# State-space layers: decay ring 8 to 16, state ring 16 to 8, sum lag 9 to 6

## The reference, cut to what matters

```
dA = exp(dt[:, :, None] * A)
h  = h * dA + (dt * u)[:, :, None] * B[:, None, :]     # over 512 time steps
y  = sum over states of h * C  +  u * D
out = x + gate * ((y * silu(z)) @ W_out)
```

## Time and profile before

| | |
|---|---|
| median of 3 runs | 2964.96 us (2961.61 to 2968.52) |
| profiled execution | 2969.68 us, span on the core 2968.0 us |
| busy share of the span | PE 82%, DVE 73%, ACT 73%, POOL 57% |
| L1038 scan | 1024 x 1209 ns, 205.5 us idle before them |
| L1121 product h * C | 1024 x 1370 ns |
| L909 decay tile, L891 scaled row | 1024 x 715 ns, 1024 x 714 ns |
| L1300, L1285 transposes and sums | 4096 each, 628.1 and 623.3 us busy |

### The profile page before, as it was taken

One profiled execution on the slowest core, in us unless ns is written; L12 is line 12 of the kernel. 1 busy time (PEld: TensorE's weight loads), 2 busy tenths in 40 slices (PEclk: granted clock), 3 DMA queues, 4 the chain that ended last, 5 costly groups with the idle time before them and its releaser, 6 DMA issues. The chain is left out here.

```text
span 2968.0 us, 44243 instructions
## 1 busy us (share of the span) xinstructions
PE 2442.6 (82%) x14532; PEld 1664.9 (56%) x14532; DVE 2178.1 (73%) x2878; ACT 2159.3 (73%) x3593; POOL 1689.8 (57%) x1365
## 2 busy tenths in 40 slices
PE   7778578898898898637888999857888888889885
PEld 4555257777677777512333333224576666677784
DVE  4443378888888898556777776615899988998983
ACT  3333389999999999513666656547989989999993
POOL 0000078888988989650111111004989889899895
PEclk9999799999999999867999999878999999999997
DMA  3100211112112111145555544111111112112121
GB/s 106 39 28 22 73 40 45 51 60 65 39 60 67 37 53 60 38 93 81 80 87 87 82 82 76 22 55 43 44 67 60 58 53 78 61 53 74 58 68 43
DMA packets 106124, 177.01 MB, mean 60 GB/s; under 512 B 10709, under 2 KB 91405, under 8 KB 97199
## 3 DMA queue, kind: packets, MB, share of 16 engines
q1 hardware_dynamic: 101679, 161.69, 21.3%
q0 software_dynamic: 4224, 12.59, 1.3%
HBM read 139.70 MB, written 34.14 MB: 59 GB/s over the span
## 5 line engine op out<-in xcount | busy, mean ns | idle before, releaser
L1121 POOL TENSOR_TENSOR l_h<-l_h,l_c_all 128x512 f32<-128x512 f32 x1024 | 1380.7, 1370 | 184.8 <-DVE l_h L1038 168.9
L1038 DVE TENSOR_TENSOR_SCAN l_h<-l_dA,l_ps_dbu 128x512 f32<-128x512 f32 x1024 | 1218.8, 1209 | 205.5 <-PE l_ps_dbu L1300 102.1
L1300 PE MATMUL l_ps_dbu<-ident,l_dub 128*128 128x128 f32 x4096 | 628.1, 276 | 151.0 <-DVE l_h L1038 79.7
L909 ACT ACTIVATE l_dA<-l_dt,l_a_neg 128x512 f32<-128x512 f32 x1024 | 731.1, 715 | 7.0 <-issue 5.2
L891 ACT ACTIVATE l_dub<-l_duT,l_b_tok 128x512 f32<-128x512 f32 x1024 | 730.4, 714 | 2.4 <-PE l_ps_dbu L1300 2.0
L1285 PE MATMUL l_ps_y<-ident,l_h 128*128 128x128 f32 x4096 | 623.3, 275 | 11.8 <-POOL l_h L1121 8.8
L1300 PEld LDWEIGHTS l_ps_dbu<-ident,l_dub 128*128 128x128 f32 x4096 | 471.0, 141 | 205.0 <-DVE l_h L1038 112.0
L1285 PEld LDWEIGHTS l_ps_y<-ident,l_h 128*128 128x128 f32 x4096 | 485.5, 142 | 130.8 <-issue 92.4
L1795 ACT ACTIVATE l_probs<-l_ring 128x512 f32<-128x512 f32 x512 | 292.8, 598 | 261.9 <-PE l_ring L1933 260.7
L1614 DVE TENSOR_REDUCE l_q_max<-l_ring 128x1 f32<-128x512 f32 x512 | 338.4, 683 | 175.6 <-PE l_ring L1926 171.8
L1933 PE MATMUL l_ring<-l_qs,l_ks 102*128 102x512 bf16 x512 | 201.5, 398 | 59.5 <-DMA l_qs<-l_m_parts 51.4
(11 more groups left out here) (248 smaller groups left out, 2949.7 us busy)
## 6 DMA issues: line engine op xcount, KB each, us to landing
l_c_all<-c_rows_dram SPq DMA_DIRECT2D x64, 1024.0 KB, 4.8
l_res<-x_dram SPq DMA_DIRECT2D x24, 512.0 KB, 6.0
parts_dram<-l_parts SPq DMA_DIRECT2D x48, 256.0 KB, 2.9
l_qs<-parts_dram SPq DMA_DIRECT2D x48, 256.0 KB
l_ks<-parts_dram SPq DMA_DIRECT2D x48, 256.0 KB
l_x_in<-x_dram SPq DMA_DIRECT2D x16, 512.0 KB, 7.3
x_dram<-l_res SPq DMA_DIRECT2D x16, 512.0 KB, 3.1
l_x_in<-in_x SPq DMA_DIRECT2D x8, 512.0 KB, 4.3
```

What stands on the lines that cost most here:

```text
L909: act.activation(dA[:, s % DA_RING, :], dt[:, p, j, :], ACT.Exp, scale=a_neg[:, j * N + n:j * N + n + 1]).then_inc(da_ok, 1)
L1038: dve.tensor_tensor_scan(h[:, h_slot(s), :], dA[:, s % DA_RING, :], ps_dbu[:, dbu_slot(s), :], 0.0, ALU.mult, ALU.add).then_inc(scan_ok, 1)
L1121: pool.tensor_tensor(h[:, h_slot(s), :], h[:, h_slot(s), :], c_all[:, (n // C_GROUP) % 2, n % C_GROUP, :], ALU.mult).then_inc(hc_ok, 1)
L1300: last = pe.transpose(ps_dbu[:, dbu_slot(s), t * P:(t + 1) * P], dub[:, DUB_SLOTS[n], t, j * P:(j + 1) * P], ident[:])
```

## The change

The decay ring gets 16 tiles in place of 8, the state ring 8 in place of 16, so the tiles' memory stays the same in sum. The sums on PE follow six units behind in place of nine, so the skip terms of a batch are at steps 6 to 9 of PE. Since 1 - DA_RING would make the first wait on scan_ok zero or negative, that semaphore gets a start of its own, SCAN_CREDIT = 16, and the waits on it by ACT, POOL and PE are raised alike.

```
 UNITS = N * JB
-DA_RING, DBU_RING, H_RING = 8, 3, 16
-SUM_LAG = 9
+DA_RING, DBU_RING, H_RING = 16, 3, 8
+SUM_LAG = 6
 CREDIT = 8
+SCAN_CREDIT = 16
...
-                        act.wait_ge(scan_ok, b * UNITS + s + 1 - DA_RING + CREDIT)
+                        act.wait_ge(scan_ok, b * UNITS + s + 1 - DA_RING + SCAN_CREDIT)
...
-                dve.sem_inc(scan_ok, CREDIT)
+                dve.sem_inc(scan_ok, SCAN_CREDIT)
...
-                        pool.wait_ge(scan_ok, b * UNITS + s + 1 + CREDIT)
+                        pool.wait_ge(scan_ok, b * UNITS + s + 1 + SCAN_CREDIT)
...
-                        pe.wait_ge(scan_ok, b * UNITS + s + 1 - dbu_back(s) + CREDIT)
+                        pe.wait_ge(scan_ok, b * UNITS + s + 1 - dbu_back(s) + SCAN_CREDIT)
```

## The result

The changed kernel takes **3105.82 us** (median of 4 runs, 3101.01 to 3112.68); the kernel before took 2966.74 beside it (4 runs). The ratio is 1.0473, with a 95% interval of 1.0447 to 1.0498: 139 us slower. The forecast was 3068, in a range from 3035 to 3105; the result lies 0.8 us above the top of the range. The profiled execution has a span of 3102.9 us, 134.9 longer than before. In the engines' programs lines stand one further on than before: the scan is L1039, the skip term L1276, the sum L1286, the transposes L1301, y_gate L1008.

A forecast was written before the change was run, and what follows sets the result against it. DVE and PE set the pace from unit 5 to 28, ACT from there to unit 4. 12 x 7.4 + 2 x 7.1 = 103 us on the median 2964.96 gave 3068 us, range 3035 to 3105 (0.80).

The forecast's parts named there:

- the stall: Units 6 to 9: PE and DVE take turns four times per batch, so scan 9 comes 8.4 us later.
- the give-back: Before unit 11: DVE's 1.09 us idle goes, no skip term being left there, so scan 11 is only 7.4 us late.
- ACT's slack absorbs it: Rival: ACT's 5.70 us of waits per batch are slack, leaving 1.7 a batch; 2985 to 3035 us; chance 0.08.
- PE is relieved: Rival: skip terms cost nothing at step 6 and the 1.09 us stall before unit 11 goes; 2950 us; chance 0.03.
- no effect: Rival: the lag and the rings are all loose; 2965 us; chance 0.02.
- The clock: I take none.: PE's new 1.9 us idle gaps in the turns: no clock loss in the centre, 27 us for the range's top.
- the top of the range: 3105 us: 10 us a batch, with one slow turn and POOL's wait.
- clock falls at every turn: Rival: half clock in all four turns of each batch, 108 us more, 3176 us; anything over 3105 has chance 0.07.
- The turn: Units 6 to 9, scan to scan through y_gate, skip term, sum and transposes: 3.82 us, where it was 1.72.
- ACT's wait at the projection: Unit 12 (L823): projection 8.3 us later; ACT's waits at L823, L844 and L836 longer by 5 to 8 us per batch.
- Layer 3: Tap relief, at most 18 us, a third (6) taken, against POOL's wait (4.5): about cancel, taken as 0.
- The wait for POOL: Layer 3, units 53 to 63: earlier sums may wait for POOL's products, 0 to 9 us in seven batches, middle 4.5.

## Why the prediction was right, and where its size was off

**Right, with numbers.** The mechanism, its place and its sign. The lag of 6 puts skip term j ahead of transposes 6 + j, PE and DVE take turns four times in each of 14 batches, and the run with the lag alone shows it to be the whole loss. The gap of PE came at 1.90 us as forecast. The decay tiles and the states came at nothing, as forecast. The batch is longer by what the stall adds, less the give-back: ACT's waits at L824 end on projections that lie behind the stall, so the rival "ACT's slack absorbs it" (2985 to 3035) is out. "PE is relieved" and "no effect" are out by the scans that wait at L1301.

**The step that failed** is "The clock: I take none." I held one row against it: the fall at 641 followed 2.30 us of waiting, and the new gaps are 1.9. They are shorter, but the clock fell all the same, in every one of the 14 windows; I had noted "four in a row" and given it no price. The changed kernel and the same with idle transposes measure it: 3105.82 and 3075.21 us, 31 apart on two chips, ratios 1.0473 and 1.0371; on the chip of the second, the lag alone took 3105.22, 30 us more. The profiles place it: 246.3 - 222.4 = 23.9 in the turns, and 51.9 - 46.1 = 5.8 from scan 9 to 11. The 27 us that I kept for the top of the range, one slow turn a batch, was about the right size; it belonged in the centre, at 3095. By the sign that I had named for it, a granted clock of 0.5 in units 6 to 9, the rival "clock falls at every turn" came true in part; its price (3176) did not: 29 of the 56 turns took 3.93 to 3.98 us, the third of the batch above among them, and the window at 619 has 1.6 us at half clock in all (twice 0.05 x 16.45).

The Trainium skill, TensorE: Matmul & The Clock Gate, section "A second HAM failure mode: psum-queue depth-cycling", says that short idle spells between groups of matmuls make the clock swing between its two levels, at a loss of throughput. The 68.1 us at half clock in these windows agree, and so does their going to 3.4 when the gaps were filled.

**The turn** was sized 3.82 us and measures 3.93 at full clock. I took the skip term at 0.89 to the next start from a row in which PE came from other work. Behind a wait it takes 752.15 to 753.14, 0.99, and 613.23 to 614.23 in the lag of 7. The likely reason is that its first weight load waits too: it starts at 752.15 together with the matmul, where in the earlier trace rows it stands at 615.44, 0.43 ahead. Over 56 turns 0.11 is 6 us. The stall at full clock was forecast at 14 x 8.4 = 118 and came to 222.4 - 95.7 = 126.7.

**The give-back** was forecast at 12 x 1.0 + 2 x 1.3 = 15 us. With the gaps filled, so at full clock, it is 63.0 - 46.1 = 16.9 from scan 9 to 11 and 3.2 from 11 to 24, 20 in all; with the clock falling, 5.8 of it is lost again. At full clock the order is then worth 126.7 - 20.1 = 107 us by the timelines and 111 by the medians, where the forecast had 103. That term was right to within 8 us.

**What I named too far on**: ACT's wait at the projection. I put the extra wait at unit 12 (L823). Projection 7 lies in the stall as well, so ACT also waits for it, 7.60 us in the batch above, and the waits at L844 that I expected to grow are gone but for the last batch's, since ACT is late by then. In sum these waits of layer 1 grew by 106.9 - 36.5 = 70 us, over 7 batches 10 each, above the 5 to 8.

**Layer 3** was taken at nothing, as a relief of the taps (up to 18 us, a third of it 6) against a new wait for POOL (4.5). All taps of both layers now:

```profile
L987 DVE SCALAR_TENSOR_TENSOR l_work<-l_conv_in,vecs,l_work 128x512 f32<-128x512 f32 x192 | 149.0, 776 | 0.8
```

That is 7.7 us less than in the earlier trace rows, so the relief came at about the third I had named. The wait for POOL came too. Before, PE's sums waited for POOL's products 11 times, 8.8 us in the whole run; now:

```profile
PE l_ps_y L1286 <- POOL l_h L1122: 29.8, 34, 2.9
```

Scans 40 to 63 of layer 3 take 262.8 us over seven batches in place of 258.4, and those of layer 1 256.9 in place of 257.1. So this term measures 4.4 us, where I had named 4.5, and the two about cancel.

**The top of the range** had one slow turn and POOL's wait, 10 us a batch, but not the longer turn. With it, 0.4 a batch, the top would have been above the result.

## What to carry to other kernels

When work is moved forward on an in-order queue, look for the first instruction in it that waits, and ask whether the engine it waits for needs anything that now stands behind it: here one unit of lag, 7 to 6, cost 113 us, and putting the needed transposes first took 107 back. When a new pattern of short TensorE gaps arises, price the clock in the centre of the forecast and not only at its edge; here it was worth about one turn per batch at half clock. This loop, balanced on three engines, left few free moves: every other place tried here for the y_gates or the sums lost 13 to 32 us.

## What was not expected of the hardware

- The clock went to 0.50 with PE idle 1.90 us at a time and at work some 2 us between, and stayed at 1.00, in 13 stretches of 14, with gaps of 0.59.
- The eight skip-term matmuls take 0.10 us longer to the next start behind a wait than behind other work: 0.99 in all 40 groups of the changed kernel that waited and ran at full clock, 0.89 in the 12 that did not wait.
- A tap took 1.40 us in place of 0.72 when POOL's product had started 0.42 us earlier, so a y_gate moved in front of a tap cost its own 0.67 us and as much again.
- Filling PE's gap ahead of the output projection kept the clock at 1.00 in the five stretches of layer 1 read here, and was worth nothing (0.9985 to 1.0013).
